# Second cross attention: the copies of TensorE-turned probabilities move from VectorE to ScalarE, to the head of its step

## What is computed

```python
x = _layernorm(x + _L0_attn_ref(...))          # windowed self attention
x = _layernorm(x + _L0_xattn_ref(ctx, ctx, x)) # one head
x = _layernorm(x + _L0_ffn_ref(...))           # 8 experts, top 2
x = _layernorm(x + _L1_attn_ref(...))          # gated state recurrence
x = _layernorm(x + _L1_xattn_ref(x, ctx, ...)) # 16 heads of 64: the block of this change
x = _layernorm(x + _L1_ffn_ref(...))           # 8 routed experts and a shared one
```

```python
xn = _layernorm(x, ln_gamma, ln_beta)
q = (xn @ w_q).reshape(B, SQ, 16, 64)
kv = context @ w_kv
...
scores = jnp.einsum('bqhd,bkhd->bhqk', q * SCALE, k)
attn = jax.nn.softmax(scores, axis=-1)
out = jnp.einsum('bhqk,bkhd->bqhd', attn, v).reshape(B, SQ, INNER)
return (out @ w_out + b_out) * jnp.tanh(gate[0])
```

## Time and profile before

| | us |
|---|---|
| median of 3 runs | 1882.11 |
| lowest, highest | 1882.07, 1885.69 |
| the profiled execution | 1884.88 |
| its span (first to last record) | 1883.0 |
| busy: PE, PEld | 1667.1, 1009.4 |
| busy: DVE | 1549.9 |
| busy: ACT | 1275.3 |
| busy: POOL | 925.5 |

### The profile page before, as it was taken

The page is one execution under the profiler, slowest core; times in us unless marked ns, Lnnn a source line. Parts: engine busy times, 40 slices in busy tenths (PEclk is TensorE's granted clock), DMA queues, the critical chain, the costliest instruction groups (busy, mean ns, idle before and its releaser), DMA issues. The chain is left out here.

```text
span 1883.0 us, 34675 instructions
## 1 busy us (share of the span) xinstructions
PE 1667.1 (89%) x10425; PEld 1009.4 (54%) x10425; DVE 1549.9 (82%) x2885; ACT 1275.3 (68%) x2106; POOL 925.5 (49%) x723
## 2 busy tenths in 40 slices
PE   4987996889957899999999999999999999994997
PEld 2654665777733344554554554454455455454886
DVE  2765785877758999999999999999999999975887
ACT  2442332877735887887888788788788888864554
POOL 3640111363335766565665656656567465421333
PEclk9997998799978999999999999999999999997998
DMA  5203884311100898988899898898888889973231
GB/s 190 95 0 127 306 332 173 85 42 45 45 34 17 180 197 174 199 182 179 190 183 190 183 190 187 178 195 182 179 199 179 188 183 185 182 135 122 47 79 29
DMA packets 632266, 281.85 MB, mean 150 GB/s; under 512 B 601852, under 2 KB 606236, under 8 KB 631452
## 3 DMA queue, kind: packets, MB, share of 16 engines
q1 hardware_dynamic: 632204, 281.10, 64.2%
HBM read 129.02 MB, written 1.05 MB: 69 GB/s over the span
## 5 line engine op out<-in xcount | busy, mean ns | idle before, releaser
L2237 DVE SCALAR_TENSOR_TENSOR xa_h<-xa_psum,xa_rinv,xa_h 128x500 f16<-128x500 f32 x672 | 452.8, 730 | 1.0 <-ACT xa_h L2445 0.7
L2445 ACT ACTIVATE xa_h<-xa_psum,xa_rinv 128x1000 f16<-128x1000 f32 x448 | 371.5, 883 | 51.8 <-DVE xa_rinv L2228 51.5
L2429 ACT ACTIVATE xa_psum<-xa_psum,xa_bias,unscale_s 128x1500 f32<-128x1500 f32 x224 | 353.2, 1577 | 7.4
L2073 PE MATMUL xa_psum<-xa_c_hi,xa_q_hi 128*128 128x500 f16 x672 | 257.4, 383 | 54.5 <-DVE xa_h L2237 50.1
L2217 DVE TENSOR_REDUCE xa_psum<-xa_psum 128x1 f32<-128x1000 f32 x224 | 269.3, 1202 | 14.2 <-PE xa_psum L2075 13.4
L2098 PE MATMUL xa_psum<-xa_prT,xa_n_hi 128*128 128x512 f16 (+1 forms) x768 | 270.8, 353 | 3.6 <-issue 1.6
L2100 PE MATMUL xa_psum<-xa_prT,xa_n_lo 128*128 128x512 f16 (+1 forms) x768 | 270.6, 352 | 0.0
L2099 PE MATMUL xa_psum<-xa_prT,xa_n_hi 128*128 128x512 f16 (+1 forms) x768 | 270.6, 352 | 0.0
L2074 PE MATMUL xa_psum<-xa_c_lo,xa_q_hi 128*128 128x500 f16 x672 | 252.7, 376 | 0.0
L2075 PE MATMUL xa_psum<-xa_c_hi,xa_q_lo 128*128 128x500 f16 x672 | 252.4, 376 | 0.0
L1939 POOL TENSOR_SCALAR xa_ctxT<-xa_ctxT,scales 128x1500 f32<-128x1500 f32 x31 | 126.3, 4073 | 166.4 <-DMA xa_ctxT<-in_ctxT 166.4
(11 more groups left out here) (328 smaller groups left out, 3630.4 us busy)
## 6 DMA issues: line engine op xcount, KB each, us to landing
ctxN<-in_ctxP SPq DMA_DIRECT2D x16, 1536.0 KB, 9.5
xa_ctxP<-in_ctxP SPq DMA_DIRECT2D x32, 768.0 KB, 4.3
ctxT<-in_ctxT SPq DMA_DIRECT2D x16, 1500.0 KB, 6.4
xa_ctxT<-in_ctxT SPq DMA_DIRECT2D x32, 750.0 KB, 4.7
moe_spread<-weight_rows SPq DMA_DIRECT2D x16, 1024.0 KB, 8.4
xa_prT<-xa_h SPq DMA_TRANSPOSE x192, 5.5
up<-in_F_up SPq DMA_DIRECT2D x1, 2048.0 KB, 7.7
down<-in_F_down SPq DMA_DIRECT2D x1, 2048.0 KB, 11.8
```

The costliest lines, as they stand in the source:

```text
L2073: nc.tensor.matmul(out, qh, c_hi[:, b, a:z], start=True, stop=False)
L2237: nc.vector.scalar_tensor_tensor(low, psum[:, bank + a:bank + z, 0:W], rinv[:, s % 2, :], high, ALU.mult, ALU.subtract).then_inc(h2_ready, 1)
L2429: nc.scalar.activation(psum[:, bank:bank + 3, 0:W], psum[:, bank:bank + 3, 0:W], ACT.Exp, bias=bias[:, s % 2, :], scale=k.unscale_s[:, :], ...
L2445: nc.scalar.activation(h[:, H_SLOT[s], 0, a * W:z * W].rearrange("p (a c) -> p a c", c=W), psum[:, bank + a:bank + z, 0:W], ACT.Identity, ...
```

## The change

`keep_turned` moves from VectorE to ScalarE. There it is the first work of a step, ahead of the bias and the exponential, and behind the high part of the unit before. The operation is an activation with the function Copy instead of a tensor copy; source, destination and the semaphore that it raises are the same. In the epilogue ScalarE makes the last three copies at its head, one after the other, ahead of the evacuations. The wait for `tok_stored` moves from VectorE (ahead of its step 3) to ScalarE (ahead of its step 2), and VectorE's wait for `xT_ready` there goes.

```diff
@@ VectorE
-            open_sems(dve, NR, *turn_kept.values())
...
-            def keep_turned(i, u, r):
-
-                dve.wait_ge(turn_ready[u], this(i, r + 1, NR))
-                nc.vector.tensor_copy(
-                    prT[:, P_SLOT[u], :, :].rearrange("p (x k) c -> p k x c", x=2)[:, r * KT // NR:(r + 1) * KT // NR, :, :],
-                    turn_bank).then_inc(turn_kept[u], 1)
...
             def step(i, s, first=False, end=False):
                 if s or not first:
                     inverse(*unit(i, s - 1))
-                at = turn_at(*unit(i, s - 1))
-                if at and (s >= UPS or not first):
-                    keep_turned(*at)
                 if s == RESIDUAL and not first:
                     residual(i - 1)
                 maximum(i, s)
...
                     x_low(3)
-                    dve.wait_ge(tok_stored, CHUNKS)
-                    dve.wait_ge(xT_ready, CHUNKS)
...
                 inverse(i, NU - 1)
-                keep_turned(i, TURNED[1], 0)
                 low_part(i, NU - 1)
-                keep_turned(i, TURNED[1], 1)
-                keep_turned(i, TURNED[1], 2)
                 residual(i)
@@ ScalarE
+            open_sems(act, NR, *turn_kept.values())
             t.open_scalar(act)
+
+            def keep_turned(i, u, r):
+
+                act.wait_ge(turn_ready[u], this(i, r + 1, NR))
+                nc.scalar.activation(
+                    prT[:, P_SLOT[u], :, :].rearrange("p (x k) c -> p k x c", x=2)[:, r * KT // NR:(r + 1) * KT // NR, :, :],
+                    turn_bank, ACT.Copy).then_inc(turn_kept[u], 1)
...
             def step(i, s, first=False, end=False):
+                at = turn_at(*unit(i, s - 1))
+                if at and (s >= UPS or not first):
+                    keep_turned(*at)
                 exponentials(i, s)
...
                     keep_features(CHUNKS - 1)
+                    act.wait_ge(tok_stored, CHUNKS)
 
             def epilogue():
+                for r in range(NR):
+                    keep_turned(PAIRS - 1, TURNED[1], r)
                 for s in range(UPS):
```

## The result

The changed kernel takes 1896.66 us (median of 4 runs, 1892.36 to 1897.21) against 1883.2 for the kernel before on the same chip: ratio 1.0065, interval 1.0046 to 1.0083. In a second job it took 1894.7 against 1883.8: 1.0051, 1.0037 to 1.0065. So it is slower, by 10 to 12 us by the two ratios (11 to 13.5 by the medians). The forecast was 1885.7 us with a range to 1895: the sign of the likeliest case was right, the size a third of what came, and the first result lies outside the range.

The account below looks back on a forecast made before the run. Bound taken as a ring of VectorE (inverse, maximum) and ScalarE (bias, exponential), with TensorE the bound in steps 7 to 9. Terms -3.5 + 0.6 + 6.0 + 0.5 = +3.6 us on 1882.1 gave 1885.7 us, range 1880 to 1895.

Parts of the forecast that it names:

- the likeliest case: Whole kernel: slower by over 0.2%, given a chance of 0.50; within 0.2% had 0.41.
- The ring with the copy at its head: VectorE and ScalarE alternating in the second cross attention: steps with a copy go from 5.01 to 4.96 us, -3.5 us.
- rival of a faster 16-bit mode: ScalarE's copy: 16-bit elements read two at a time, step 4.53 us, -34 us, about 1848 us; chance 4%.
- the one of strides: ScalarE's copy into the turned tile: rearranged output makes it 0.2 us later or longer, 1889 or 1904 us; chance 10%.
- The output product in step 7: TensorE, bank 7: the product waits for the pair's first copy, 0.40 us in each of 15 pairs, +6.0 us.
- The next turn: TensorE behind the copy of the round before: allows a 4.77 us step against ScalarE's 4.96, so nothing is added.
- turn chain: Waking TensorE exceeds the 0.19 us in hand; copy, turn, scores, maximum become the ring: 1890 to 1896 us; chance 8%.
- First and last pair: The written-out pairs: a step with a copy lasted 4.89 us, so 4.96 loses 0.07 in 8 steps, +0.6 us.
- the tail: The last turn's second round at the end of the phase waits for its copy until 1683.40, +0.5 us.
- Edits at nothing: Moved waits on x_tok and xT, earlier low parts and VectorE's extra idle time: no effect on the time.

Follow-up runs that it names:

- e1: The changed kernel, but the first copy of unit 4 (step 7) is made by VectorE again; 1884.19 us, 0.9997 of the kernel before.
- e2: The changed kernel, but the third copy of unit 11 (step 2 of the next pair) is on VectorE again; 1889.46 us, 1.0030 of the kernel before.
- e4: The changed kernel, but every pair's projection reads the first pair's inputs, at constant addresses; 1891.08 us, 1.0043 of the kernel before.
- e5: The changed kernel, but all six copies on ScalarE stand one step sooner, ahead of the high parts; 1850.42 us, 0.9826 of the kernel before.
- e6: The kernel before, all copies on VectorE, but each behind the maximum of its step instead of ahead; 1883.29 us, 0.9994.

## Why the prediction was wrong, point by point

- **The ring with the copy at its head.** Right in mechanism and size. The copy took 1.02 us, its successor started 952.73 - 951.83 = 0.90 us after it (0.92 forecast), and the step came to 4.96 us as forecast. Of the gain of 0.05 us in each of five steps 0.12 us a pair came instead of 0.25, since step 0 took 5.04 us and the others gained 0.03 to 0.05. The Trainium skill (page "ScalarE: Activation LUTs", section "What ACT_TABLE_LOAD costs") gives 186 ns and 0.833 ns an element, fp32 and bf16 alike. That makes an estimated 1.04 us, and the trace agrees with 1.02. The rival of a faster 16-bit mode did not occur, nor the one of strides.
- **The output product in step 7.** Right in mechanism, too small in size: 0.40 us was taken for the delay, and the steps from 7 to 10 grew by 15.13 - 14.60 = 0.53 us. In this pair the copy ended at 979.95 + 1.02 = 980.97, the loads and the product started 0.13 us later, and the product then took 982.54 - 981.10 = 1.44 us up to the scores instead of 1.34. The term was +6.0 and measures 15 x 0.53 = +8.0 us; e1 takes it away.

```profile
979.95 1.02 ACT L2385 ACTIVATE xa_prT<-xa_psum 128x1024 f16<-128x1024 f16 x1
981.10 1.60 PE L2133 MATMUL xa_psum<-value_out,xa_on 128*128 128x128 f32 x12 [0.26 <-ACT xa_prT L2385]
982.54 0.37 PE L2073 MATMUL xa_psum<-xa_c_hi,xa_q_hi 128*128 128x500 f16 x1
```

- **The next turn: "nothing is added, with 0.19 us in hand".** This is the step that failed. It reckoned the cover for a turn and let the projection and the transpose pass under the same number. For the turns it held: steps 1, 2 and 12, behind a turn, stayed at ScalarE's pace; for the transpose it held too, step 13 stayed at 4.40 us. The projection starts 0.38 us after the copy instead of 0.06 and, at 958.84 - 958.19 = 0.65 us up to the scores, is longer than a turn (0.46), so the scores of unit 3 start at 958.84, 0.92 us ahead of their inverse, where they would have to be 1.46 - 0.28 = 1.18 us ahead. The missing 0.26 us are what step 3 grew by: 14 x 0.26 = +3.6 us, and e2 takes them away. The rival "turn chain" named this mechanism with 8%, in the wrong member of the chain. That its 1890 to 1896 us lie near the result is luck: it charges five steps of a pair, and one paid. e4 shows that about two thirds of the loss come from operands that depend on the pair.
- **First and last pair.** +0.6 us and the tail +0.5 were forecast. The eight steps with a copy took 0.8 us more and the tail 0.6, both nearly as forecast. The last pair took 1.16 us more, 0.55 of it in step 8, which belongs to the term above. The first took 1.55 us more, 0.23 of it in step 2 and 1.17 in step 4, neither of which was foreseen. Both come before the first copy of the phase, in step 7; the 1.17 us are a lower clock of TensorE (last section), and no run ties them to the copies.
- **Edits at nothing.** Nothing of the moved waits shows at the place of ScalarE's new wait: step 2 of e5, which has it too, lasts what it did before (6.51 and 6.49 us). One gain was not foreseen and is not explained: step 10 is 0.12 us shorter in the changed kernel and in e1 to e5, but not in e6. It lies on VectorE between the last of the moments and the maximum, which start 0.23 us apart before and in e6, and 0.12 us apart in the changed kernel and in e1.

In sum over the phase: forecast +3.6, measured in the trace +9.8 and 0.6 in the tail, +10.4. The loop gives 14 x (0.53 + 0.26 - 0.12 - 0.12 - 0.04 for the remaining steps) = +7.1 us, the written-out pairs +2.7. Of the gap of 6.8 us to the forecast, 2.0 and 3.6 us are the two terms on TensorE, and 1.4 us steps 2 and 4 of the first pair. The steps with a copy gained 1.8 us less than forecast; step 10 and the remaining steps gave back about 2.2 that were not forecast.

## What to carry to other kernels

Before a piece of work moves between engines that hand each other results in a ring, mark two things for each place it could have: whether the ring stands still for it, and when it ends against the first user queued behind it, each user by itself. Here the same 96 copies on the same engine were worth +11 us at the head of the step and -34 us in the gap in which that engine waited for the inverse, one step sooner. A total that doesn't move can hide a gain and a loss of the same size; compare the steps before concluding that something costs nothing.

## What the runs showed of the hardware

- A wait on TensorE that is released late costs more than its lateness when the work behind it has operands that depend on the loop's counter: 0.38 us from release to first matmul against 0.26 with fixed ones and 0.06 for a turn.
- TensorE's granted clock falls to half for some microseconds in the first pair of some of these kernels, and what that costs depends on where it falls. Busy time and granted clock in one stretch: changed kernel, the kernel before, e2.

```profile
624.00:631.00 7.00, 5.37 (x23) 2.57 (x24) 5.72 (x10) 5.61 (x10) 6.76 (x3) 0.51 0.99 237
```
```profile
624.00:631.00 7.00, 6.50 (x42) 3.16 (x40) 6.55 (x13) 6.97 (x13) 6.76 (x4) 0.76 1.00 238
```
```profile
624.00:631.00 7.00, 4.74 (x30) 1.88 (x30) 6.60 (x14) 6.76 (x13) 6.76 (x4) 1.00 1.06 255
```

  In both traces of the changed kernel TensorE has stood 2.7 us without a matmul and the scores of step 4 start at 0.50 (the 1.2 GHz level). Nine matmuls of 500 columns take 3.9 us instead of 2.1, and step 4 takes 5.44 us instead of 4.27. In the kernel before the clock is 1.00 (2.4 GHz) behind 2.4 us without a matmul, and falls to 0.50 only at the end of those scores, from 625 to 628 us; there it costs 0.09 us (step 5: 4.36 instead of 4.27), as TensorE even so stands 0.48 us before its next scores. e1 shows the same (4.33); e2 to e6 show no such fall. It is not the order of work that decides: e4 has that of the changed kernel. The traces part earlier: ahead of the first inverse, TensorE stands 2.1 us for GpSimd in both traces of the changed kernel and starts again at full clock (500 columns in 0.39 us), and 4.1 us in all the others, starting at half clock (0.60 us). Why was not settled.
- ScalarE reads 1,024 fp16 elements from PSUM in 1,016 to 1,024 ns, as long as fp32 ones (1,026 ns); VectorE copies them in 690 ns; its maximum over 1,000 fp32 elements, another operation, takes 1,202 ns.
